# Macaron transformer on one core: exponential, scan and weight rests of the feed-forwards' routing rearranged

## Chip, cores and metric

One Trainium2 chip (trn2), one of its cores. The metric is device time in microseconds of one execution. Engines: TensorE (PE, its weight loads PEld), VectorE (DVE), ScalarE (ACT), GpSimd (POOL), SyncE (SP, which issues the DMAs here).

## What is computed

A tensor of 8 x 512 tokens with 128 channels passes six residual blocks: F0, A0, F0 (layer 0), F1, A1, F1 (layer 1). Each adds its result to x, the feed-forwards with a factor of 0.5. The change touches the four feed-forwards.

```python
# layer 0: gated, 8 experts and 2 shared, hidden 256, the best 2 of 8
shared = sum(_ffn(xf, sw1[i], sw2[i], sw3[i]) for i in range(2))
logits = xf @ router_w.T + expert_bias
rw, sel = jax.lax.top_k(logits, 2)
rw = jax.nn.softmax(rw, axis=-1)
combine = jnp.einsum('tk,tke->te', rw, one_hot(sel, 8))
out = shared + sum(combine[:, e] * _ffn(xf, w1[e], w2[e], w3[e]))   # silu(x w1) * (x w3) w2

# layer 1: relu squared, 8 experts, hidden 512, the best 2 of 8, with a capacity
oh_t = one_hot(top_idx, 8).transpose(1, 0, 2).reshape(2 * N, 8)      # N = 4096 tokens
pos = jnp.cumsum(oh_t, axis=0)
rank = jnp.sum((pos - 1) * oh, axis=-1)
valid = rank < 1280
out = sum over k of expert_out[top_idx[k]] * softmax(top_logits)[k] * valid[k]
```

## The kernel before

The program is a row of phases, P (loads, first norm), F0a, A0, F0b, F1a, A1, F1b; all engines but SyncE meet at a barrier between two phases (`barrier`, line 115), and each engine's instructions stand in an order written out by hand. Order between engines comes from semaphores alone. x lies in SBUF as `X` (32 tiles of 128 tokens) and transposed as `XT`.

`ffn_phase` (line 851) builds a feed-forward. It has a routing stage and then a loop over 8 chunks of 512 tokens.

Routing, on VectorE (`route_vector`, line 531): 32 tiles x 8 logits, 256 elements per partition, are handled at once. Two rounds (lines 539 to 551) find the largest and the second largest logit; the difference of the two maxima goes into `ex` (line 558); the one-hots are cast to bf16 (`oh_b`, line 560). `route_scalar` (line 602) takes the exponential on ScalarE; lines 563 to 567 make the two probabilities of it. In layer 1, TensorE counts with two matmuls (`route_tensor`) how many tokens of a tile went to each expert, and VectorE sums these counts with eight scans of 64 elements, one per expert (line 577), forms ranks and masks by the capacity (lines 580 to 589). Lines 594 to 598 weight, add the two choices and halve the sum, which gives `cw`. TensorE transposes `cw` (`turn_weights_tensor`, line 620), ScalarE copies it out (`keep_weights_scalar`, line 626; in layer 1 with a square root), and SyncE writes it to memory (line 520) and reads it back repeated over the partitions as `cwb`, half a chunk at a time (line 526). The routing's scratch lies in `cwb` itself in layer 1, and in `dn1` in layer 0.

Products are kept near fp32 precision by splitting each operand into a top part and a rest (three matmuls for each product): `XS` holds both parts of a chunk of XT, `dn_hi`/`dn_lo` those of the down weights, `up1_hi`/`up1_lo` those of layer 1's up weights, whose raw form is loaded by DMA at the phase's start into the buffer `h`. In the kernel before, ScalarE makes the top parts of the weights (lines 906 and 908) ahead of the exponential, and GpSimd makes both parts of the first XS (`split_gpsimd`, lines 230 and 232) and all rests of weights (lines 930 and 933).

The loop: TensorE runs three matmuls for an up-projection (lines 251 to 253; six in layer 0), and, `LAG` columns later, three for the down-projection (268 to 270), each waiting for its semaphore in order. In layer 0, ScalarE applies Silu (line 330), VectorE multiplies (408), GpSimd multiplies with `cwb` (477), ScalarE and VectorE split the result (322, 401). In layer 1, VectorE takes relu times `cwb` (line 445) and so needs `cwb` for its first column, ScalarE squares and copies (359, 364), VectorE subtracts (431), and GpSimd does both parts for every fourth column. GpSimd also splits the next chunk's XS. `norm_scalar` (lines 176, 177) copies a transposed chunk twice, into `xT_c` and into XT, and `norm_logits_tensor` (line 164) waits for both copies before its matmuls (line 168) read `xT_c`.

Of the kernel before, what the change touches and what calls it, by code (L numbers as in the profile page):

```python
# [34 lines left out]
def macaron(nc, x, alpha, w_qkv0, bias_rows0, wo0, wo0_t, wfc0, router0, expert_bias, up0, down0,  # L35
            w_qkv1, wo1, router1, up1, down1, out, stop_after=99):
    ctx = ExitStack()
    with ctx:
# [37 lines left out]
        dn_top, dn_split = sem("dn_top"), sem("dn_split")  # L76
        weights_out = sem("weights_out")
# [86 lines left out]
        def norm_logits_tensor(eng, s, i, lay, bank=7):  # L164
            eng.wait_ge(s["xt_copied"], 2 * i + 4)
            eng.wait_ge(s["lg_copied"], i + 1)
            for t in range(TPC):
                last = eng.matmul(ps[:, bank, t * E:(t + 1) * E], xT_c[:, t * P:(t + 1) * P], rw[lay][:, :],
                                  start=True, stop=True)
            last.then_inc(s["lg_done"], 1)  # L170
# [63 lines left out]
        def ffn_tensor(eng, s, lay, XS, hl, yT, w_hi, w_lo, dn_hi, dn_lo, nxt):  # L234
# [21 lines left out]
            def down(c, p, done, j):  # L256
                e, hb = divmod(j, HB)
                n = c * N + j
                if lay == 0:
                    eng.wait_ge(s["lo_done"], n + 1)  # L260
                elif on_pool(j):
                    eng.wait_ge(s["lo_pool"], c * pool_part(N) + pool_part(j + 1))
                else:
                    eng.wait_ge(s["lo_done"], c * own_part(N) + own_part(j + 1))
                if j == 0 and done == 2:
                    eng.wait_ge(s["x_added"], c - 1)
# [40 lines left out]
        def gated_scalar(eng, s, h, hl, yT, nxt):  # L307
# [4 lines left out]
            eng.preload_act_table(ACT.Silu)  # L312
# [150 lines left out]
        def gated_gpsimd(eng, s, XS, h, cwb, loads, nxt):  # L463
# [3 lines left out]
            def chunk(c, p, done):  # L467
                if done:
                    eng.wait_ge(s["up_done"], c * N)
# [15 lines left out]
        def squared_gpsimd(eng, s, XS, h, hl, nxt):  # L485
# [3 lines left out]
            def chunk(c, p, done):  # L489
                if done:  # L490
                    eng.wait_ge(s["up_done"], c * N)
# [39 lines left out]
        def route_vector(eng, buf, n, lay, m0):  # L531
            work, oh, oh_b, m, ex, pr, rank, tot, cum, incr = buf
# [5 lines left out]
            for k in range(2):  # L538
                eng.tensor_reduce(m[:, k, :], src[:, :, :], AX.X, ALU.max)
                eng.drain()  # L540

# [26 lines left out]
            eng.drain()  # L568
            if lay == 1:
# [17 lines left out]
                for k in range(2):  # L587

                    eng.scalar_tensor_tensor(out=oh[:, k].rearrange("p t e -> p (t e)"),
                                             in0=rank[:, k].rearrange("p t e -> p (t e)"), scalar=float(CAP),  # L590
                                             in1=oh[:, k].rearrange("p t e -> p (t e)"), op0=ALU.is_lt, op1=ALU.mult)
# [5 lines left out]
            eng.drain()  # L597
            eng.tensor_scalar(cw[:, :, :, :].rearrange("p c e t -> p c t e"),
                              work[:, 2].rearrange("p (c t) e -> p c t e", t=TPC), 0.5, None, ALU.mult)
            eng.drain().then_inc(step, 1)  # L600

        def route_scalar(eng, buf, n):
            ex = buf[4]
            eng.wait_ge(step, n + 2)
# [26 lines left out]
        def route_buffers(scratch, oh_b):  # L631
            taken = [0]

            def b(*shape):
# [5 lines left out]
                if len(shape) == 2:  # L640
# [3 lines left out]
                    b(E, 2, TILES), b(E, 2 * TILES), incr]  # L644
# [206 lines left out]
        def ffn_phase(name, lay, nxt):  # L851
# [9 lines left out]
            with ExitStack() as st:  # L861
# [17 lines left out]
                def body(block):  # L879
# [13 lines left out]
                    def _(eng):  # L893
# [4 lines left out]
                        eng.wait_ge(dn_split, number + 1)  # L898
                        ffn_tensor(eng, s, lay, XS, hl, yT, w_hi, w_lo, dn_hi, dn_lo, nxt)
# [18 lines left out]
                    def _(eng):  # L918
                        route_vector(eng, buf, n0, lay, m0)
# [28 lines left out]
        def attn0():  # L948
# [10 lines left out]
            with ExitStack() as st:  # L959
# [43 lines left out]
                def body(block):  # L1003
# [299 lines left out]
                    def _(eng):  # L1303
# [77 lines left out]
                        def chunk(c, p, done):  # L1381
                            first = done == 0
                            for n in range(UNITS):
# [43 lines left out]
                                if n == 5:  # L1427
                                    norm_logits_tensor(eng, s, c, nxt, SPARE)
# [18 lines left out]
                        for n in range(LAST):  # L1447
# [9 lines left out]
                            if n == 5:  # L1457
                                norm_logits_tensor(eng, s, B, nxt, SPARE)
# [7 lines left out]
                        norm_logits_tensor(eng, s, B + 1, nxt, SPARE)  # L1466
# [688 lines left out]
```

## Time and profile before

| | us |
|---|---|
| median of 3 runs | 3185.7 |
| lowest, highest | 3185.64, 3187.7 |
| profiled execution | 3189.26 |
| its span, first to last instruction | 3187.5 |

| engine | busy us | share of the span |
|---|---|---|
| PE | 2611.3 | 82% |
| PEld | 1734.8 | 54% |
| DVE | 2328.8 | 73% |
| ACT | 2261.4 | 71% |
| POOL | 1904.3 | 60% |

The page's shares are means over seven phases with different limits. What a routing stage costs has to be read from the stretch between a phase's barrier and its first up-projection, by engine. Times in a trace are from the span's start. In a row of the timeline, the brackets at its end tell how long the engine was idle before it and who released it.

### The profile page before, as it was taken

The page shows a single profiled execution, that of the slowest core. Times are in us where ns is not written, and L with a number is a line of the kernel's source. Part 1 is how long each engine was busy: PE and PEld are TensorE (multiplying, and loading weights), DVE is VectorE, ACT ScalarE, POOL GpSimd, SP SyncE. Part 2 cuts the span into 40 slices and gives each one's busy share as a digit, 9 for nine tenths or more (in the row PEclk, how much of TensorE's full clock was granted, in tenths as well). Part 3 has the DMA queues.
Part 4 walks back from the last instruction along what each step waited for, and adds up shares of the span by engine and source line. Part 5 has one row for each costly group of instructions (what it writes and reads, how often), then busy time and mean ns, then how long its engine had stood idle before and what let it go on. Part 6 is the DMA issues. An engine that isn't in the chain of part 4 may idle for free. (4 is left out here: it accounts for less than half of the span.)

```text
span 3187.5 us, 42265 instructions
## 1 busy us (share of the span) xinstructions
PE 2611.3 (82%) x12174; PEld 1734.8 (54%) x12208; DVE 2328.8 (73%) x4338; ACT 2261.4 (71%) x2559; POOL 1904.3 (60%) x1486
## 2 busy tenths in 40 slices
PE   4999958999789996799985778777787787469998
PEld 3877745555478774678872223232232232158887
DVE  5677746666466675898877687787787878378887
ACT  2555526777545554577764999999999999557776
POOL 2766667777456675444444666666766767344444
PEclk9999979999899998899996666676767666679999
DMA  3111100000011111111100000000000000111111
GB/s 114 54 40 53 39 1 1 2 1 1 1 55 54 53 39 66 55 54 40 45 21 1 0 0 1 1 1 1 1 1 1 1 1 1 53 51 44 53 39 53
DMA packets 13588, 86.72 MB, mean 27 GB/s; under 512 B 2176, under 2 KB 4224, under 8 KB 4224
## 3 DMA queue, kind: packets, MB, share of 16 engines
q1 hardware_dynamic: 13440, 84.96, 7.2%
q8 instruction: 67, 1.10, 0.1%
q14 instruction: 81, 0.66, 0.1%
HBM read 82.33 MB, written 2.62 MB: 27 GB/s over the span
## 5 line engine op out<-in xcount | busy, mean ns | idle before, releaser
L1743 POOL TENSOR_TENSOR A_Y<-A_Y,A_U 128x2048 f32<-128x2048 f32 x86 | 389.9, 4555 | 226.8 <-ACT A_U L1786 226.8
L1819 DVE TENSOR_SCALAR A_U<-ps 128x1024 f32<-128x1024 f32 x256 | 309.3, 1219 | 126.1 <-POOL A_Y L1743 62.4
L1825 DVE SCALAR_TENSOR_TENSOR A_U<-ps,A_U 128x1024 f32<-128x1024 f32 x256 | 311.4, 1216 | 58.2 <-PE ps L1955 58.2
L1955 PE MATMUL ps<-A_QT,A_KT 9*128 9x512 f32 x512 | 181.4, 705 | 195.8 <-DVE A_U L1825 163.3
L477 POOL TENSOR_TENSOR F0b_h<-F0b_h,dn 128x512 f32<-128x512 f32 x128 | 211.9, 1660 | 123.7 <-DVE F0b_h L408 123.5
L477 POOL TENSOR_TENSOR F0a_h<-F0a_h,dn 128x512 f32<-128x512 f32 x128 | 212.0, 1661 | 117.4 <-DVE F0a_h L408 117.2
L513 POOL TENSOR_TENSOR gated<-half_neg 128x1 f32<-128x1 f32 x179 | 37.7, 210 | 397.8 <-ACT F1a_h L359 178.3
L1743 POOL TENSOR_TENSOR dn<-dn,A_U 128x2048 f32<-128x2048 f32 x42 | 190.2, 4553 | 112.6 <-ACT A_U L1786 112.6
L1955 PEld LDWEIGHTS ps<-A_QT,A_KT 9*128 9x128 f32 x512 | 66.0, 254 | 335.5 <-DVE A_U L1825 238.4
L1265 DVE CUSTOM_DVE_ANT_0 ps<-ps,A_mask 128x256 f32<-128x256 f32 (+1 forms) x512 | 185.1, 423 | 84.4 <-PE ps L1335 78.8
L1786 ACT ACTIVATE A_U<-A_U 128x2048 f32<-128x2048 f32 (+1 forms) x96 | 236.5, 2464 | 0.0
L1927 PE MATMUL ps<-A_Y,A_VA 128*32 128x512 f32 x688 | 229.1, 800 | 5.8 <-DVE A_OT L1725 3.0
L445 DVE SCALAR_TENSOR_TENSOR F1b_h<-ps,F1b_cwb 128x512 f32<-128x512 f32 x256 | 176.1, 688 | 51.9 <-PE ps L253 34.4
L330 ACT ACTIVATE F0b_h<-ps 128x512 f32<-128x512 f32 x160 | 95.8, 599 | 161.7 <-PE ps L253 161.7
L359 ACT ACTIVATE F1a_h<-F1a_h 128x512 f32<-128x512 f32 x256 | 158.3, 625 | 71.9 <-DVE F1a_h L445 70.9
L1044 POOL TENSOR_SCALAR A_KZ<-A_KT,A_own 128x512 fp32r<-128x512 f32 x132 | 204.5, 1566 | 5.6 <-issue 5.6
L330 ACT ACTIVATE F0a_h<-ps 128x512 f32<-128x512 f32 x160 | 95.8, 599 | 155.4 <-PE ps L253 155.4
L359 ACT ACTIVATE F1b_h<-F1b_h 128x512 f32<-128x512 f32 x256 | 161.0, 629 | 61.6 <-DVE F1b_h L445 57.4
L1944 PE MATMUL ps<-A_QT,A_KT 28*128 28x512 f32 x512 | 167.5, 671 | 42.2 <-DVE A_U L1819 38.2
L1785 ACT ACTIVATE A_Y<-A_U 128x2048 f32<-128x2048 f32 (+1 forms) x64 | 159.4, 2490 | 51.6 <-DVE A_U L1825 51.4
L445 DVE SCALAR_TENSOR_TENSOR F1a_h<-ps,F1a_cwb 128x512 f32<-128x512 f32 x256 | 173.0, 684 | 24.9 <-PE ps L253 15.2
L408 DVE TENSOR_TENSOR F0b_h<-F0b_h,ps 128x512 f32<-128x512 f32 x160 | 109.9, 687 | 103.1 <-ACT F0b_h L330 102.5
(365 smaller groups left out, 8366.6 us busy)
## 6 DMA issues: line engine op xcount, KB each, us to landing
dn<-weight_rows SPq DMA_DIRECT2D x32, 1024.0 KB, 4.7
F1a_cwb<-weight_rows SPq DMA_DIRECT2D x16, 1024.0 KB, 4.7
F1b_cwb<-weight_rows SPq DMA_DIRECT2D x16, 1024.0 KB, 4.7
dn<-in_down SPq DMA_DIRECT2D x2, 2048.0 KB, 12.1
stage<-in_up SPq DMA_DIRECT2D x1, 2560.0 KB, 9.4
X<-in_x SPq DMA_DIRECT2D x1, 2048.0 KB, 8.4
F1a_h<-in_up SPq DMA_DIRECT2D x1, 2048.0 KB, 7.5
F1b_h<-in_up SPq DMA_DIRECT2D x1, 2048.0 KB, 7.7
```

Source lines behind the costliest of these rows:

```text
L330: eng.activation(h[:, j % ring, :], ps[:, (j * G) % 4, :], ACT.Silu).then_inc(s["pre_done"], 1)
L359: eng.activation(z, z, ACT.Square).then_inc(s["sq_done"], 1)
L445: eng.scalar_tensor_tensor(out=h[:, j % ring, :], in0=ps[:, j % 4, :], scalar=0.0, in1=cwb[:, j // HB, :], op0=ALU.max, op1=ALU.mult).then ...
L477: eng.tensor_tensor(z, z, cwb[:, r // HB, :], ALU.mult).then_inc(s["weighed"], 1)
L1044: last = eng.tensor_scalar(KZ[:, g % 2, j, :], KT[:, g, :].bitcast(F32), own[:, j:j + 1], None, ALU.mult)
L1265: last = eng.tensor_tensor_reduce(part, part, mask[:, w0:w1], -1.0, 3e38, ALU.add, ALU.min, QA[:, p, t, 4 * g + 2 * i + b, 3 * HD:3 * HD + ...
L1743: eng.tensor_tensor(flat(y_slot(m, h)), flat(y_slot(m, h)), flat(Um[:, h % UR]), ALU.add).then_inc(s["t_ready"], 1)
L1786: eng.activation(u, u, ACT.Sqrt).then_inc(s["s_ready"], 2 if joined else 1)
L1819: eng.tensor_scalar(u_step(n), d_pair(n), 0.0, None, ALU.max).then_inc(s["dp_vector"], 1)
L1825: eng.scalar_tensor_tensor(out=u, in0=g_pair(), scalar=CLAMP, in1=u, op0=ALU.min, op1=ALU.mult).then_inc(s["u_ready"], 1)
L1927: last = eng.matmul(ps[j:j + 32, OUT, :], VA[:, v0:v0 + 32], y_slot(m, h)[:, kt, :], start=(kt == 0), stop=(kt == TPC - 1))
L1955: last = eng.matmul(ps[:, 4 + b, :], KT[r:r + 9, pair, kt * P:(kt + 1) * P], QT[r:r + 9, pair, :], start=True, stop=True)
```

## The change

- `ex`, the difference of the maxima, is computed inside the second round, and its semaphore step comes there.
- ScalarE's order in a feed-forward becomes: table load for Exp, copy of the first chunk into XS, (layer 0: copy of dn_hi), exponential, table load (Sqrt or Silu), (layer 1: copies of up1_hi and dn_hi when their DMAs are in), copy of the turned weights.
- VectorE makes, after the whole routing, the rests of XS, of up1 (layer 1) and of the down weights; GpSimd makes none of them. GpSimd's first `split_gpsimd`, for the second chunk, waits for the first up-projection.
- The eight scans become one over 512 elements, whose multiplier is 0 at each expert's first element and 1 elsewhere (`restart`, set by GpSimd at the start of a layer 1 phase).
- Casts to `oh_b` are made in layer 1 alone. The weighting multiplies move ahead of the wait for TensorE's counts; the capacity mask is applied to their result. The halving moves into line 563, where it costs no instruction, and line 598 goes.
- TensorE waits for `dn_split` at its first down-projection instead of ahead of the loop.
- `norm_logits_tensor` waits for the first of the two copies only, in the feed-forwards.

```diff
-        def norm_logits_tensor(eng, s, i, lay, bank=7):
-            eng.wait_ge(s["xt_copied"], 2 * i + 4)
+        def norm_logits_tensor(eng, s, i, lay, bank=7, copies=1):
+            eng.wait_ge(s["xt_copied"], 2 * i + 2 + copies)
...
+                if j == 0 and done == 0:
+                    eng.wait_ge(dn_split, number + 1)
...
             def chunk(c, p, done):
-                if done:
-                    eng.wait_ge(s["up_done"], c * N)
+                eng.wait_ge(s["up_done"], c * N if done else 1)
                 split_gpsimd(eng, s, XS, (c + 1) % B, 1 - p)
...
+                if k == 1:
+                    eng.tensor_tensor(ex[:, 0, :], m[:, 1, :], m[:, 0, :], ALU.subtract).then_inc(step, 1)
...
-            eng.tensor_tensor(ex[:, 0, :], m[:, 1, :], m[:, 0, :], ALU.subtract).then_inc(step, 1)
-            for k in range(2):
-                eng.tensor_copy(oh_b[:, k].rearrange("p e t -> p t e"), oh[:, k])
+            if lay == 1:
+                for k in range(2):
+                    eng.tensor_copy(oh_b[:, k].rearrange("p e t -> p t e"), oh[:, k])
             eng.drain().then_inc(step, 1)
             eng.wait_ge(step, n + 3)
-            eng.tensor_scalar(ex[:, 2, :], ex[:, 1, :], 1.0, None, ALU.add)
+            eng.tensor_scalar(ex[:, 2, :], ex[:, 1, :], 1.0, 2.0, ALU.add, ALU.mult)
...
+            for k in range(2):
+                eng.tensor_tensor(work[:, k], oh[:, k], be(pr[:, k, :]), ALU.mult)
             if lay == 1:
                 eng.wait_ge(step, n + 4)
...
-                for e in range(E):
-                    eng.tensor_tensor_scan(cum[:, e, :], ones_f[:, 0:2 * TILES], tot[:, e].rearrange("p k t -> p (k t)"),
-                                           0.0, ALU.mult, ALU.add)
+                eng.wait_ge(restart_ready, n_restart)
+                eng.tensor_tensor_scan(cum[:, :, :].rearrange("p e n -> p (e n)"), restart[:, 0, :],
+                                       tot[:, :, :, :].rearrange("p e k t -> p (e k t)"), 0.0, ALU.mult, ALU.add)
...
-            for k in range(2):
-                eng.tensor_tensor(work[:, k], oh[:, k], be(pr[:, k, :]), ALU.mult)
             eng.drain()
-            eng.tensor_tensor(work[:, 2], work[:, 0], work[:, 1], ALU.add)
-            eng.drain()
-            eng.tensor_scalar(cw[:, :, :, :].rearrange("p c e t -> p c t e"),
-                              work[:, 2].rearrange("p (c t) e -> p c t e", t=TPC), 0.5, None, ALU.mult)
+            eng.tensor_tensor(cw[:, :, :, :].rearrange("p c e t -> p c t e"),
+                              work[:, 0].rearrange("p (c t) e -> p c t e", t=TPC),
+                              work[:, 1].rearrange("p (c t) e -> p c t e", t=TPC), ALU.add)
...
                     @block.scalar
                     def _(eng):
+                        eng.preload_act_table(ACT.Exp)
+                        eng.activation(XS[:, 0, 0, :], XT[:, 0:S], ACT.Copy).then_inc(xs_top, 1)
+                        if lay == 0:
+                            eng.activation(dn_hi[:, :, :, :], dn_raw[:, :, :, :], ACT.Copy).then_inc(dn_top, 1)
+                        route_scalar(eng, buf, n0)
                         if lay == 1:
+                            eng.preload_act_table(ACT.Sqrt)
                             eng.wait_ge(load["up1"], 16 * load_number)
                             eng.activation(w_top, w_raw, ACT.Copy).then_inc(up1_top, 1)
                             eng.wait_ge(load["dn1"], 16 * load_number)
-                        eng.activation(dn_hi[:, :, :, :], dn_raw[:, :, :, :], ACT.Copy).then_inc(dn_top, 1)
-                        route_scalar(eng, buf, n0)
+                            eng.activation(dn_hi[:, :, :, :], dn_raw[:, :, :, :], ACT.Copy).then_inc(dn_top, 1)
+                        else:
+                            eng.preload_act_table(ACT.Silu)
                         keep_weights_scalar(eng, cw_t, m0, lay)
...
                     @block.vector
                     def _(eng):
-                        route_vector(eng, buf, n0, lay, m0)
+                        route_vector(eng, buf, n0, lay, load_number)
+                        eng.wait_ge(xs_top, number + 1)
+                        eng.tensor_tensor(XS[:, 0, 1, :], XT[:, 0:S], XS[:, 0, 0, :].bitcast(F32),
+                                          ALU.subtract).then_inc(s["split_done"], 1)
+                        if lay == 1:
+                            eng.wait_ge(up1_top, load_number)
+                            eng.tensor_tensor(w_rest, w_raw, w_top.bitcast(F32), ALU.subtract).then_inc(up1_split, 1)
+                        eng.wait_ge(dn_top, number + 1)
+                        eng.tensor_tensor(dn_lo[:, :, :, :], dn_raw[:, :, :, :], dn_hi[:, :, :, :].bitcast(F32),
+                                          ALU.subtract).then_inc(dn_split, 1)
...
                     @block.gpsimd
                     def _(eng):
                         if lay == 1:
-                            eng.wait_ge(up1_top, load_number)
-                            eng.tensor_tensor(w_rest, w_raw, w_top.bitcast(F32), ALU.subtract).then_inc(up1_split, 1)
-                        split_gpsimd(eng, s, XS, 0, 0)
-                        eng.wait_ge(dn_top, number + 1)
-                        eng.tensor_tensor(dn_lo[:, :, :, :], dn_raw[:, :, :, :], dn_hi[:, :, :, :].bitcast(F32),
-                                          ALU.subtract).then_inc(dn_split, 1)
+                            flags = buf[9][:, 0, :]
+                            eng.memset(flags, 1.0)
+                            eng.drain()
+                            eng.memset(flags.rearrange("p (e n) -> p e n", e=E)[:, :, 0:1], 0.0)
+                            eng.drain().then_inc(restart_ready, 1)
```

## Rows read from the trace of the kernel before

**Rows 1.** Stages: stretch, us, busy us of PE, PEld, DVE, ACT, POOL, clock, DMA share, GB/s.
```profile
50.40:67.40 17.00, 0.00 (x0) 0.00 (x0) 14.84 (x22) 2.57 (x2) 9.52 (x5) 1.00 0.00 0
1251.80:1290.40 38.60, 0.63 (x1) 0.13 (x2) 25.68 (x36) 10.03 (x5) 21.22 (x6) 0.50 0.27 109
1640.00:2776.70 1136.70, 824.33 (x3217) 342.74 (x3215) 851.67 (x995) 1021.75 (x414) 721.88 (x441) 0.68 0.00 1
2776.70:2815.70 39.00, 0.63 (x1) 0.13 (x2) 26.97 (x37) 8.63 (x4) 21.22 (x6) 0.50 0.27 108
2824.40:3187.00 362.60, 352.92 (x1556) 291.21 (x1556) 307.98 (x456) 279.28 (x456) 167.99 (x206) 0.98 0.13 49
```

**Rows 2.** Timeline of DVE in F0a: start, us, engine, line, operation, idle before.
```profile
51.07 0.42 DVE L539 TENSOR_REDUCE dn<-logits 128x32 f32<-128x256 f32 x1 [0.63 <-PEq L651]
...
53.98 5.34 DVE L548 TENSOR_TENSOR dn<-dn 128x256 f32<-128x256 f32 x1
...
63.15 1.27 DVE L560 CAST F0a_r_ohb<-dn 128x256 bf16<-128x256 f32 x2
64.75 0.18 DVE L563 TENSOR_SCALAR dn<-dn 128x32 f32<-128x32 f32 x1 [0.32 <-ACT dn L605]
...
67.03 0.40 DVE L598 TENSOR_SCALAR cw<-dn 128x256 f32<-128x256 f32 x1
...
71.43 0.69 DVE L408 TENSOR_TENSOR F0a_h<-F0a_h,ps 128x512 f32<-128x512 f32 x1 [4.00 <-ACT F0a_h L330]
```

**Rows 3.** Timeline of POOL in F0a's routing.
```profile
53.47 5.57 POOL L933 TENSOR_TENSOR F0a_dn_lo<-dn,F0a_dn_hi 128x2560 fp32r<-128x2560 f32 x1 [0.34 <-ACT F0a_dn_hi L908]
```

**Rows 4.** Timeline of PE in F0a: its first up-projection matmul.
```profile
67.86 0.78 PE L251 MATMUL ps<-F0a_xs,up_lo 128*128 128x512 f32 x1
```

**Rows 5.** Timeline of DVE in F1a.
```profile
1252.42 0.42 DVE L539 TENSOR_REDUCE F1a_cwb<-logits 128x32 f32<-128x256 f32 x1 [0.65 <-PEq L651]
...
1257.41 0.42 DVE L548 TENSOR_TENSOR F1a_cwb<-F1a_cwb 128x256 f32<-128x256 f32 x1
...
1270.00 2.48 DVE L563 TENSOR_SCALAR F1a_cwb<-F1a_cwb 128x32 f32<-128x32 f32 x1 [10.71 <-ACT F1a_cwb L605]
...
1274.08 11.74 DVE L577 TENSOR_TENSOR_SCAN F1a_cwb<-ones_f,F1a_cwb 128x64 f32<-128x64 f32 x8
...
1298.27 1.89 DVE L445 SCALAR_TENSOR_TENSOR F1a_h<-ps,F1a_cwb 128x512 f32<-128x512 f32 x3 [7.88 <-DMA F1a_cwb<-weight_rows]
```

**Rows 6.** Timeline of ACT in F1a.
```profile
1264.81 3.62 ACT L908 ACTIVATE F1a_dn_hi<-dn 128x4096 fp32r<-128x4096 f32 x1 [1.27 <-DMA dn<-in_down]
1268.45 1.28 ACT L605 ACT_TABLE_LOAD   x1
1269.74 0.23 ACT L605 ACTIVATE F1a_cwb<-F1a_cwb 128x32 f32<-128x32 f32 x1
...
1291.19 0.38 ACT L626 ACTIVATE F1a_cw_t<-ps 128x256 f32<-128x256 f32 x1 [19.93 <-PE ps L620]
```

**Rows 7.** Line 577 in F1b: count, ns shortest/median/longest, first and last start.
```profile
L577 DVE TENSOR_TENSOR_SCAN F1b_cwb<-ones_f,F1b_cwb x8: 258/260/7952, 2800.4 to 2810.8; 128x64 f32<-128x64 f32 x8
```

**Rows 8.** Chain of waits through F1b's start: start, us, what.
```profile
2789.85 3.62 ACT F1b_dn_hi L908
...
2816.46 0.39 ACT F1b_cw_t L626
...
2824.39 0.70 DVE F1b_h L445
...
2831.06 0.43 PE ps L269
2831.48 0.23 PE ps L270
```

**Rows 9.** Timeline of DVE in P: the 5120-element subtraction.
```profile
44.61 5.49 DVE L841 TENSOR_TENSOR up_lo<-stage,up_hi 128x5120 fp32r<-128x5120 f32 x1 [1.35 <-ACT up_hi L809]
```

**Rows 10.** Timeline of PE at F0b's end: the last logits matmuls.
```profile
1249.67 1.87 PE L168 MATMUL ps<-rw,xT_c 128*128 128x8 f32 x8 [1.17 <-ACT XT L177]
```

More of the change, by code:

```diff
@@ L76, in macaron @@
         dn_top, dn_split = sem("dn_top"), sem("dn_split")
+        xs_top, restart_ready = sem("xs_top"), sem("restart_ready")
         weights_out = sem("weights_out")
@@ L232, in split_gpsimd, with ffn_tensor @@
             eng.tensor_tensor(lo, xt, hi.bitcast(F32), ALU.subtract).then_inc(s["split_done"], 1)
-        def ffn_tensor(eng, s, lay, XS, hl, yT, w_hi, w_lo, dn_hi, dn_lo, nxt):
+        def ffn_tensor(eng, s, lay, XS, hl, yT, w_hi, w_lo, dn_hi, dn_lo, nxt, number):
             U, HB, G = ffn_shape(lay)
@@ L311, in gated_scalar @@
                 norm_credits_scalar(eng, s)
-            eng.preload_act_table(ACT.Silu)
             def top(c, done, j):
@@ L489, in chunk @@
             def chunk(c, p, done):
-                if done:
-                    eng.wait_ge(s["up_done"], c * N)
+                eng.wait_ge(s["up_done"], c * N if done else 1)
                 split_gpsimd(eng, s, XS, (c + 1) % B, 1 - p)
@@ L528, in weights_sync, with route_vector @@
                         .then_inc(weights_in[half], 16)
-        def route_vector(eng, buf, n, lay, m0):
-            work, oh, oh_b, m, ex, pr, rank, tot, cum, incr = buf
+        def route_vector(eng, buf, n, lay, n_restart):
+            work, oh, oh_b, m, ex, pr, rank, tot, cum, restart = buf
             def be(a):
@@ L587, in route_vector @@
                 for k in range(2):
-                    eng.scalar_tensor_tensor(out=oh[:, k].rearrange("p t e -> p (t e)"),
+                    eng.scalar_tensor_tensor(out=work[:, k].rearrange("p t e -> p (t e)"),
                                              in0=rank[:, k].rearrange("p t e -> p (t e)"), scalar=float(CAP),
-                                             in1=oh[:, k].rearrange("p t e -> p (t e)"), op0=ALU.is_lt, op1=ALU.mult)
-                eng.drain()
-            for k in range(2):
-                eng.tensor_tensor(work[:, k], oh[:, k], be(pr[:, k, :]), ALU.mult)
+                                             in1=work[:, k].rearrange("p t e -> p (t e)"), op0=ALU.is_lt, op1=ALU.mult)
             eng.drain()
-            eng.tensor_tensor(work[:, 2], work[:, 0], work[:, 1], ALU.add)
-            eng.drain()
-            eng.tensor_scalar(cw[:, :, :, :].rearrange("p c e t -> p c t e"),
-                              work[:, 2].rearrange("p (c t) e -> p c t e", t=TPC), 0.5, None, ALU.mult)
+            eng.tensor_tensor(cw[:, :, :, :].rearrange("p c e t -> p c t e"),
+                              work[:, 0].rearrange("p (c t) e -> p c t e", t=TPC),
+                              work[:, 1].rearrange("p (c t) e -> p c t e", t=TPC), ALU.add)
             eng.drain().then_inc(step, 1)
@@ L603, in route_scalar @@
             ex = buf[4]
-            eng.wait_ge(step, n + 2)
+            eng.wait_ge(step, n + 1)
             eng.activation(ex[:, 1, :], ex[:, 0, :], ACT.Exp).then_inc(step, 1)
@@ L643, in route_buffers @@
             return [b(3, TILES, E), b(2, TILES, E), oh_b, b(3, TILES), b(3, TILES), b(2, TILES), b(2, TILES, E),
-                    b(E, 2, TILES), b(E, 2 * TILES), incr]
+                    b(E, 2, TILES), b(E, 2 * TILES), b(1, E * 2 * TILES)]
         out_w1 = sb("out_w1", [P, D])
@@ L897, in _ @@
                             eng.wait_ge(up1_split, load_number)
-                        eng.wait_ge(dn_split, number + 1)
-                        ffn_tensor(eng, s, lay, XS, hl, yT, w_hi, w_lo, dn_hi, dn_lo, nxt)
+                        ffn_tensor(eng, s, lay, XS, hl, yT, w_hi, w_lo, dn_hi, dn_lo, nxt, number)
                         barrier(eng, b0)
@@ L1427, in chunk @@
                                 if n == 5:
-                                    norm_logits_tensor(eng, s, c, nxt, SPARE)
+                                    norm_logits_tensor(eng, s, c, nxt, SPARE, 2)
                                 if n == 6:
@@ L1457, in _ @@
                             if n == 5:
-                                norm_logits_tensor(eng, s, B, nxt, SPARE)
+                                norm_logits_tensor(eng, s, B, nxt, SPARE, 2)
                         eng.wait_ge(s["lg_copied"], B + 2)
@@ L1465, in _ @@
                         norm_turn_tensor(eng, s, B + 1, SPARE)
-                        norm_logits_tensor(eng, s, B + 1, nxt, SPARE)
+                        norm_logits_tensor(eng, s, B + 1, nxt, SPARE, 2)
                         barrier(eng, b0)
```

## Prediction

> **What bounds the kernel now.** I read the stage table first, to see where TensorE stands still, then the timelines of those stages, then the chain of waits through one of them. The four feed-forward phases each open with a routing stage in which TensorE does nothing of weight: 17.0 us in F0a (F0b repeats it, instruction for instruction), 38.6 us in F1a, 39.0 us in F1b [rows 1]. Behind it the loops over the chunks are TensorE's: 352.92 of 362.60 us busy in F1b [rows 1], with back-to-back matmuls of 0.23 us at full clock [rows 8]. So whatever the prologue is shortened by, TensorE's first up-projection starts earlier and the phase ends earlier by the same amount; nothing in the loop can take it back, since the loop's own pace is unchanged.
>
> In the prologue the reader should see two kinds of lost time. First, lock-like stalls on VectorE. In F0a line 548 takes 5.34 us, from 53.98 to 59.32 [rows 2], and its twin in F1a takes 0.42 us [rows 5]; GpSimd's subtraction for dn_lo runs from 53.47 to 59.04 [rows 3], and the stalled instruction ends 0.28 us after it. In F1 the same happens to line 563 (2.48 us for 32 elements) and to the first of the eight scans (11.74 us for the group in F1a [rows 5]; in F1b one scan is 7952 ns where the shortest is 258 ns [rows 7]). Second, the exponential: in the F1 phases it stands on ScalarE's queue behind two copies of 3.62 us that wait for the weights' DMAs, the second of which ends at 1268.43 in F1a [rows 6] and 2793.47 in F1b [rows 8]; VectorE idles 10.71 us for it in F1a [rows 5].
>
> The Trainium skill, SBUF — State Buffer, section "Who interferes with whom", says that a VectorE instruction with two SBUF inputs and a GpSimd instruction that reads SBUF exclude each other for a whole instruction, and that the one issued first wins. By that rule the 5.34 us are 0.42 of work and the rest waiting; the rows agree to 0.28 us.
>
> **The change, part by part.**
>
> *GpSimd leaves the routing (all phases).* Its two weight subtractions and the first chunk's split go to VectorE and ScalarE, and its first split now waits for the first up-projection. So both rounds of the arg-max run as they do in F1a, where GpSimd was idle: line 539 starts at 1252.42, line 548 of round two ends at 1257.83, 5.41 us [rows 5]. The difference `ex` (32 elements, about 0.26 us with its gap, an estimate between line 563's 0.18 [rows 2] and a 256-element 0.42) now stands inside it: 5.7 us.
>
> *F0a.* Before: 51.07 to the end of line 598 at 67.43, 16.4 us [rows 2]. After: 5.7, no casts of oh_b (line 560, 1.27 us, on the path as TensorE doesn't use them here), no wait for the exponential (see below), then lines 563 to 596, which are 64.75 to 67.03 less a gap, 2.3 us [rows 2]; line 598 (0.40 and its gap) is folded into the addition. That is 8.0 us, so cw stands at 59.1 instead of 67.43: 8.35 us earlier. TensorE then waits for VectorE's new XS subtraction, 512 elements: by line 841, 5.49 us for 5120 elements [rows 9], 1.07 ns per element, so 0.55 and an overhead: 0.7 us where the old start came 0.34 us behind the transposes' start and needed nothing. Cost 0.45. The dn_lo subtraction (2560 elements, 2.75 us by the same rate) runs from 59.9 to 62.7; TensorE only asks for it at the first down-projection, and VectorE's own next work, line 408, came 3.57 us behind TensorE's first matmul (67.86 [rows 4] to 71.43 [rows 2]), so 60.0 plus 3.57, 63.5: covered by 0.8 us. Were the cover gone it would cost at most 2.75. Gain of F0a: 7.9 us. Bounds 6.5 to 8.4.
>
> ScalarE's new order in F0a is table load, XS copy, dn_hi copy, exponential. Two of its durations stand in the stage row (2.57 us for the dn_hi copy and the exponential [rows 1]); with a 512-wide copy of about 0.6 (an estimate from 3.62 us for 4096 elements and an overhead) and a table load of 1.28 [rows 6] it is done some 4.5 us in, at 55.5, while VectorE asks for it at 56.8. In hand: 1.3 us. The Trainium skill, ScalarE: Activation LUTs, "What ACT_TABLE_LOAD costs", gives 1283 ns for the load and another 1380 ns of drain; by it the exponential would come at 56.9, and the sum would be 0.1 us worse per F0 phase. Against it stands that the load in F1a began 0.02 us behind a copy and ended where the exponential began, at 1269.74 [rows 6].
>
> *F0b.* Same instructions, same stalls, 7.9 us. Further, the last logits matmul waits for one copy instead of two: it stood at 1249.67 behind line 177's copy [rows 10], and now starts one overlapped copy, 0.5 us, earlier. In the loop this wait is hidden behind TensorE's queue. 8.4 us.
>
> *F1a.* Two rounds 5.7 from 1252.42, casts 1.27 (they feed TensorE's two ranking matmuls here): 1259.4. The exponential now needs only the copy of XS ahead of it and is done about 1256.5; no wait. The tail before, from line 563's end at 1272.48 to the stage's end at 1290.4 [rows 1], was 17.9 us, of which 11.74 are scans [rows 5]: 6.2 left, less 0.5 for line 598, plus 0.2 for an unstalled line 563, is 5.9. The one scan over 512 elements: no row shows one. A 512-wide plain pass at 1.07 ns is 0.7; eight times the shortest scan is 8 x 0.258 [rows 7] = 2.1. I take 1.2, as the shortest scan stands above a plain instruction of its size and eight fixed costs become one. Routing ends at 1259.4 + 5.9 + 1.2 = 1266.6 instead of 1290.4. TensorE's ranking matmuls run beside the weighting multiplies, which are moved in front of the wait for just that.
>
> Now what is next late. (a) ScalarE: its copy of dn_hi holds it until 1268.43 [rows 6], so the weights leave then and not at 1267.3; from line 626's start to line 445's start were 7.08 us (1291.19 [rows 6] to 1298.27 [rows 5]), two DMAs through memory: weights there at 1275.5. (b) VectorE: after 1266.6 come 0.7 for XS, 4.4 for up1's rests and 4.4 for dn_lo (4096 elements each at 1.07 ns): free at 1276.2. Both subtractions lie beside the weights' travel, as (a) and (b) tie within 1 us. (c) TensorE starts its ups once up1's rests are there, at 1271.7, and has the first four banks full 12 x 0.43 us later [rows 8], at 1276.9, while line 445 needs them one by one; not late. Line 445 starts at 1276.3 against 1298.27: 22.0 us. The restart flags are two GpSimd memsets at the stage's start, 10 us ahead of the scan; they cost nothing unless they hold up VectorE's first instructions, at most 1 us.
>
> *F1b.* Same routing, 14.2 us, from 2777.3 (its stage begins at 2776.7 [rows 1]): cw at 2791.5. ScalarE is free only at 2793.47 [rows 8], and from line 626 to line 445 were 7.93 us (2816.46 to 2824.39 [rows 8]): weights at 2801.4; VectorE free at 2801.1. Gain 2824.39 - 2801.4 = 23.0 us.
>
> *TensorE's clock.* Before, TensorE filled its banks, stalled for the weights, and then ran 0.43 us per matmul (1.2 GHz) until 2831.3, when it rose to 0.23 us (2.4 GHz) [rows 8]. Now the filling ends just as line 445 begins, so the clock should be up by then. From 2825.1 to 2831.3 are 14 matmuls, 3.3 us at full clock: 2.8 us to be had at most, none at least. The ramp of the first columns through ScalarE and VectorE takes part of it back; I take 1.0 in each F1 phase.
>
> **Sum.** 7.9 + 8.4 + 23.0 + 24.0 = 63.3 us. The profiled execution was 3189.3 us (span 3187.5) and would be 3126.0; the median of the runs shown is 3.6 us lower, so 3185.7 - 63.3 = 3122.4 us.
>
> **Rivals.**
> *1. The weights' travel becomes the bound and is longer than before.* The row loads now follow the 2 MB loads by 4 to 10 us instead of 25. Line 626 to 445 took 7.08 and 7.93 us; two to four us more in each F1 phase gives 3126 to 3131. For: only the travel is now behind ScalarE's last copy in F1b. Against: the weights' loads have landed by then (2789.85 [rows 8]). Chance 0.12.
> *2. GpSimd's postponed split collides with VectorE.* By the rule cited above the two block one another, and GpSimd's pair of instructions is 1.98 us (9.52 less 5.57, for two pairs [rows 1, 3]). It becomes ready one up-projection into dn_lo's subtraction, is held until that ends, and then may hold VectorE's first hl rest: up to 1.3 us in each F1 phase, 3125. Without the rule nothing. Chance 0.10.
> *3. The stalls are not GpSimd's.* Then lines 548 and 577 keep their long instructions: F0 gains 2 us each, F1 some 12 each, total 28, 3158 us. Against it the matched ends (0.28 us). Chance 0.03.
> *4. Slower: the clock is granted less in F1b.* F1b follows A1, in which the granted clock was 0.68 over 1136.7 us; F1b had 0.98 [rows 1]. The changed F1b begins its TensorE work 19 us sooner behind A1 and without the pause. If it were held at 0.68, its 362.6 us would be 362.6 x 0.98/0.68 = 522, plus 160, net 3282. It decides once the loop's mean falls below 0.98 x 362.6/(362.6+63) = 0.83. Against: in F1b the clock rose 15.6 us after the routing stage's end (2815.7 [rows 1] to 2831.3 [rows 8]), stall included. Chance 0.02.
> *5. The exponential or the flags hold the routing after all* (ScalarE's table loads, late flags): 1 us in each phase, 3126. Chance 0.05.
> *6. More than summed*: the whole clock term and a shorter travel, 67 to 70 us, 3116 to 3119. Chance 0.10.
>
> **How the numbers follow.** Forecast, 3119 to 3126: 0.58. Rivals 1, 2, 5 and 6 lie between 3116 and 3131, together 0.37; 3 and 4 lie far away. The bounds of the terms add up to some 55 to 69 us. The range takes them in with a little: 3114 to 3133. What a measurement can tell from no change is 0.2%, 6.4 us, a tenth of the gain; only rival 4 crosses it: faster 0.97, same 0.01, slower 0.02.
>
> **What would show it.** In the changed profile: no VectorE instruction of the routing over 1 us but the scan and the casts; line 548's twin 0.42 in F0a; the exponential ended before VectorE reaches its wait; TensorE's first up-projection 8 us earlier relative to the stage's start in F0, and the first use of the weights 22 to 23 us earlier in F1, with about 0.2 us between VectorE's last subtraction and it. Wrong would be: a VectorE wait of several us for the weights' DMA behind the subtractions (rival 1), rests of hl over 1 us at the loop's start (2), 0.43 us matmuls far into a loop (4).

## The result

The changed kernel takes 3134.5 us (median of 4 runs, 3131.6 to 3135.5) against 3186.1 us before (median of 4): a ratio of 0.9835, 95% interval 0.9822 to 0.9848, or 51.7 us less. The forecast was 3122.4 us, 63.3 us less. Its profiled execution took 3135.5 us (before 3189.3), span 3133.8. One execution of one kernel below (b_vector_rests) took 4715.4 us in a slower state and enters no comparison.

What was forecast for the routing stages came to within half a microsecond. The stage table of the changed kernel, columns as in [rows 1]:

```profile
50.40:59.20 8.80, 0.03 (x1) 0.03 (x1) 6.85 (x18) 5.54 (x5) 0.00 (x0) 1.00 0.00 0
1235.90:1250.80 14.90, 1.07 (x3) 0.17 (x3) 12.59 (x30) 8.56 (x6) 0.64 (x2) 0.50 0.70 282
2747.80:2763.10 15.30, 1.08 (x3) 0.18 (x3) 12.61 (x30) 9.10 (x6) 0.64 (x2) 0.50 0.68 275
```

From the barrier to the finished `cw`, 17.0, 38.6 and 39.0 us [rows 1] have become 8.8, 14.9 and 15.3 us, and GpSimd is idle in them but for the flags (0.64 us in each layer 1 stage). VectorE in F0a and in F1a (timeline: start, us, engine, line, operation, idle before), answering [rows 2] and [rows 5]:

```profile
56.10 0.42 DVE L550 TENSOR_TENSOR dn<-dn 128x256 f32<-128x256 f32 x1
...
63.54 0.69 DVE L410 TENSOR_TENSOR F0a_h<-F0a_h,ps 128x512 f32<-128x512 f32 x1 [0.91 <-ACT F0a_h L332]
...
1236.57 0.42 DVE L539 TENSOR_REDUCE F1a_cwb<-logits 128x32 f32<-128x256 f32 x1 [0.65 <-PEq L651]
...
1246.00 1.22 DVE L581 TENSOR_TENSOR_SCAN F1a_cwb<-F1a_cwb 128x512 f32<-128x512 f32 x1
...
1250.05 0.62 DVE L597 TENSOR_TENSOR cw<-F1a_cwb 128x256 f32<-128x256 f32 x1
1250.79 0.69 DVE L927 TENSOR_TENSOR F1a_xs<-XT,F1a_xs 128x512 fp32r<-128x512 f32 x1
1251.40 4.42 DVE L931 TENSOR_TENSOR up_lo<-F1a_h,up_hi 128x4096 fp32r<-128x4096 f32 x1
1255.74 4.42 DVE L933 TENSOR_TENSOR F1a_dn_lo<-dn,F1a_dn_hi 128x4096 fp32r<-128x4096 f32 x1
1260.07 1.88 DVE L447 SCALAR_TENSOR_TENSOR F1a_h<-ps,F1a_cwb 128x512 f32<-128x512 f32 x3
```

No routing instruction is held (line 550 is 0.42 us where its twin took 5.34), and the first use of the weights comes 1260.07 - 1236.57 = 23.5 us behind the routing's first instruction, where it was 45.85 us [rows 5]. VectorE comes to it with no idle time: its own rests were the last, the weights were there.

The missing time is in F1a. From VectorE's first routing instruction of one feed-forward to that of the next (and to the span's end), in us:

| kernel | F0a and A0 | F0b | F1a and A1 | F1b |
|---|---|---|---|---|
| before | 816.6 | 384.8 | 1524.9 | 410.2 |
| changed | 808.5 | 377.1 | 1511.9 | 385.3 |
| gained | 8.1 | 7.7 | 13.0 | 24.9 |
| forecast | 7.9 | 8.4 | 23.0 | 24.0 |

F1a's prologue gained 22.35 us (45.85 less 23.5), and its first addition to x came 22.5 us earlier. The two phases together gained 13.0, so 9.5 us were given back behind it: 8.3 in F1a's loop, as follows, and 1.2 behind F1a's last addition (1115.5 us up to F1b's routing, before 1114.3), nearly all of it A1. The starts of VectorE's addition to x (line 380, after it 382) stand 45.5 us apart all through F1a's loop before, and 45.5, 45.6, **49.6**, 45.5, **49.8**, 45.5 us in the changed kernel. VectorE and TensorE in the first long one:

```profile
1439.17 0.69 DVE L447 SCALAR_TENSOR_TENSOR F1a_h<-ps,F1a_cwb 128x512 f32<-128x512 f32 x1 [1.81 <-PE ps L254]
1442.63 0.69 DVE L433 TENSOR_TENSOR F1a_hl<-F1a_h,F1a_hl 128x512 fp32r<-128x512 f32 x1 [2.77 <-issue]
...
1443.38 0.50 PE L271 MATMUL ps<-F1a_hl,F1a_dn_lo 128*128 128x512 f32 x1 [2.14 <-DVE F1a_hl L433]
```

```profile
1437.75:1441.00 3.25, 3.25 (x16) 2.55 (x14) 0.69 (x1) 1.01 (x2) 2.87 (x4) 1.00 0.88 323
1441.00:1443.40 2.40, 0.26 (x3) 0.02 (x1) 0.77 (x2) 0.25 (x1) 0.87 (x1) 1.00 0.01 3
1443.40:1447.40 4.00, 4.00 (x11) 3.15 (x12) 4.00 (x7) 3.26 (x6) 0.25 (x1) 0.57 0.00 0
```

"<-issue" is the row to see: VectorE stands 2.77 us and waits for nothing that the profile shows. TensorE runs out of work for 2.14 us, and its granted clock then is 0.57 over 4 us (mostly 1.2 GHz) where it was 1.00. The period is 4.1 us longer in all; how much of that is the clock is shown by b_pad117 below. It happens at each of the two jumps back of VectorE's chunk loop, which holds 300 instructions of the program.

### The profile page after: what moved, and what is told of

Same layout as the page of the kernel before. It is cut to its first block and busy times, and to the rows that moved or that the text cites. A ratio compares the mean times of both kernels' runs of the same rounds, so it can differ in the third digit from the quotient of the medians.

```text
span 3133.8 us, 42282 instructions
## 1 busy us (share of the span) xinstructions
PE 2620.4 (84%) x12208; PEld 1739.4 (56%) x12208; DVE 2308.5 (74%) x4326; ACT 2266.4 (72%) x2566; POOL 1857.2 (59%) x1476
```

## Experiments

### Is it the place of the code?

The change leaves VectorE with 11 instructions fewer ahead of F1a's loop. Five kernels shift VectorE's code and nothing else, by semaphore increments at its head in phase P (the number stands in the name); a sixth writes its loops out.

```diff
                 @block.vector
                 def _(eng):
+                    for _i in range(16):
+                        eng.sem_inc(spare, 1)
                     eng.wait_ge(load["x"], 16)
```

> The changed kernel with 16 semaphore increments put at the head of VectorE's queue in phase P, where it idles 9.16 us for x. They do no work and only shift all later VectorE code by 16 instructions. Theory A (code position): in the changed kernel VectorE stands still for 2.8 us with nothing to wait for at each of the two jumps back in F1a's chunk loop, and instruction packets of 8192 bytes are loaded there; the shorter code ahead of the loop (11 instructions) has moved the loop across one more block boundary. 16 more put it back: the two stalls go, all chunk periods of F1a are 45.5 us, F1a with A1 is 8 us shorter, and the kernel takes some 3126 us. Theory B (the stalls come from the new order of work itself, say from cwb's loads or GpSimd's postponed split): nothing changes, 3134 us.

Measured: 3123.1 us, ratio 0.9802 (0.9786 to 0.9818). Every period of F1a's loop is 45.5 or 45.6 us, and no wait for "issue" is left there. F0a starts where it did (50.98 us, 51.01 without the increments), so the increments themselves cost nothing. The theory of the code's position holds, the new order of the work isn't the cause.

> The same with 100 increments. Two versions of theory A differ here. A1, blocks of 128 instructions (8192 bytes, the size of the instruction packets on the queue that serves VectorE; 64 bytes each) of which a loop can use three: the loop's start falls at 89 to 99 in a block of 128, 300 instructions then touch four blocks, the stalls stay: 3134 us. A2, the page Runtime: NRT and Kernel Launch of the Trainium skill, section Instruction fetch mechanics, which has blocks of 256 instructions and two of them at hand: 300 instructions from 89 to 99 touch two blocks, no stall: 3126 us. Theory B: 3134 us, and then a_pad16 also.

Measured: 3125.0 us, 0.9806 (0.9790 to 0.9823), periods 45.9 us at the jumps. As a time that looks like the expectation's version A2 (blocks of 256), but the DMA view says otherwise. Two queues carry instructions: q8 has 67 packets in every kernel here, and q14 has 81 before and 91 in the changed kernel and changes with VectorE's code. Instruction packets on q14, over the last three chunk periods of F1a's loop (columns: packets, MB, share of the DMA engines), in the changed kernel, in a_pad100, in a_pad118 and in a_pad128, the same line in each:

```profile
q14 instruction: 6, 0.05, 0.1%
```

For the same stretch of a_pad16 and of the kernel before, the view has no instruction packet at all. So with 100, blocks of the loop are loaded anew in each turn too, and only the price is lower: 0.4 us for each jump. (F0a starts 1.1 us later here, for the increments.)

> The kernel before with 117 increments at the same place, which put F1a's VectorE loop at the same place in a block of 128 as the changed kernel has it (11 short of before's), and far from a boundary of 256. A1: the kernel before gets the same two stalls, F1a's periods become 45.5 and twice 49.7 us, 3186 + 8 = 3194 us. A2 and B: 3186 us. The increments themselves are hidden behind the 9.16 us wait.

Measured: 3196.0 us, 1.0028 (1.0018 to 1.0037), periods 49.6 and 48.3 us at the jumps, six instruction packets. The kernel before can be given the changed kernel's loss. 2.8 of the 9.3 us are the increments (117 take longer than the idle time for x, 9.2 us; F0a starts at 53.9 instead of 51.1), which the expectation had as hidden.

The second of its jumps tells what the clock cost. VectorE and TensorE there, and the four us behind it (columns as in [rows 1]):

```profile
1576.83 0.69 DVE L432 TENSOR_TENSOR F1a_hl<-F1a_h,F1a_hl 128x512 fp32r<-128x512 f32 x1 [2.83 <-issue]
...
1577.58 0.50 PE L269 MATMUL ps<-F1a_hl,F1a_dn_lo 128*128 128x512 f32 x1 [2.17 <-DVE F1a_hl L432]
```

```profile
1577.50:1581.50 4.00, 3.92 (x17) 3.28 (x18) 4.00 (x8) 3.16 (x6) 0.14 (x1) 1.00 0.00 0
```

Both engines stand as long as in the changed kernel, but the granted clock stays at 1.00, and the period is 2.8 us longer and not 4.1. So the stop itself costs 2.8 us and the fallen clock some 1.3 more. It fell behind the other five such stops (the changed kernel's, a_pad128's and b_pad117's first: 0.57 to 0.67 over 4 us); why not behind this one stays open.

> The changed kernel with 128 increments at VectorE's head. If the period of the block is 128 instructions (8192 bytes), F1a's loop stands as in the changed kernel itself and its two long periods (49.6 and 49.8 us) come back: 3134 us and at most 1 to 3 us more for the increments. If the period is 256, or the position doesn't matter, periods of 45.5 us and 3124 us.

Measured: 3138.6 us, 0.9845 (0.9828 to 0.9861), periods 49.9 and 49.4 us. F0a starts 3.9 us later for the increments; without them it is the changed kernel's time. The stalls come back after 128 instructions. By the times alone a divisor of 128 would do as well; the packets of 8192 bytes speak for 128.

> The changed kernel with 118 increments: F1a's loop starts 10 instructions earlier in its block than in the changed kernel, so 11 to 21 ahead of the next block boundary, where the changed kernel stands 1 to 11 ahead of it (4.1 us for each jump back) and a_pad100 29 to 39 ahead (0.4 us, though the blocks are loaded again there too). Theory A1, refined: the loop touches four blocks in all three, and what is lost depends on how soon behind the jump's target the next block, which isn't there either, is needed. So the two long periods lie between 45.9 and 49.8 us, by the distance nearer the long end: 48 to 49 us, 3131 us. If the cost is one of yes or no by the number of blocks, 49.7 or 45.5 us.

Measured: 3127.9 us, 0.9812 (0.9796 to 0.9828), of which 3.0 us are the increments (F0a starts at 54.05), periods 45.9 and 46.3 us, though the blocks are loaded again. The expected 48 to 49 us was wrong: 10 instructions from the place where a jump costs 4.1 us, nearly all of the price is gone. VectorE at the same jump in a_pad118:

```profile
1440.56 0.69 DVE L448 SCALAR_TENSOR_TENSOR F1a_h<-ps,F1a_cwb 128x512 f32<-128x512 f32 x1 [1.85 <-PE ps L255]
1441.17 0.68 DVE L434 TENSOR_TENSOR F1a_hl<-F1a_h,F1a_hl 128x512 fp32r<-128x512 f32 x1
```

Both kernels idle some 1.8 us at the jump. The row names TensorE, but in a_pad16, which loads nothing, the longest wait around there is 0.49 us, so this is most likely the load of the target's block; TensorE's lead covers it. Only the changed kernel has a second stop at this jump, 2.77 us, one instruction later (a_pad118 has one of 0.59 us at its other jump). That a second block is missing there fits the packets; why 10 instructions more between target and block boundary hide nearly all of it was not measured.

One rival can be set aside from the traces. SyncE's row loads for `cwb` fill the DMA engines just as the blocks are fetched (share 0.88 from 1437.75 to 1441.00 above), so the stop might be a queue behind them. But VectorE also stands 2.38 us at A0's jump, where the share is 0.02:

```profile
636.44 0.36 DVE L1279 CUSTOM_DVE_ANT_0 ps<-ps,A_mask 128x192 f32<-128x192 f32 x1 [2.38 <-issue]
```

```profile
634.00:637.00 3.00, 2.69 (x19) 1.50 (x19) 0.62 (x4) 1.53 (x4) 0.00 (x0) 1.00 0.02 5
```

The row loads can be at the root of a few tenths of the 2.77 us, not of the stop.

The Trainium skill, Runtime: NRT & Kernel Launch, "Instruction fetch mechanics", has this mechanism: sequential prefetch, and a taken jump whose target isn't at hand stalls for a DMA. It gives blocks of 16 KiB or 256 instructions, two at hand. For VectorE the runs differ: packets of 8192 bytes (0.05 MB for six) and a period of 128. A count of the instructions gives the loop's start in its block up to a constant, and 11 values of that constant make all runs fit one rule: where the loop touches three blocks of 128 nothing is loaded again, where it touches four it is. A0's loop has 481 instructions on VectorE and so always touches four or more, which fits its stops in both kernels. A1's loop has 673 and yet shows no wait for "issue" over 0.3 us in the changed kernel; why was not followed up.

The loops written out on VectorE (A0, F1a, F1b):

```diff
-        def all_chunks(eng, chunk):
+        def all_chunks(eng, chunk, flat=False):
             chunk(0, 0, 0)
             chunk(1, 1, 1)
+            if flat:
+                for c in range(2, B):
+                    chunk(c, c % 2, 2)
+                return
...
-            all_chunks(eng, chunk)
+            all_chunks(eng, chunk, True)
...
-                        all_chunks(eng, chunk)
+                        all_chunks(eng, chunk, True)
```

> The changed kernel with VectorE's chunk loops of A0, F1a and F1b written out (no jump back on VectorE; the other engines keep theirs). Theory A: no jump, no stall. F1a's two go (8.2 us), and the two of 2.35 us in A0, which both kernels have, go too, worth up to 4.7 us: 3121 to 3126 us. Theory B: 3134 us.

Measured: 3120.3 us, 0.9792 (0.9775 to 0.9808), the fastest here, 66 us under the kernel before. F0a and A0 take 803.9 us where the changed kernel took 808.5; 4.0 of the 4.6 us lie behind F0a's last addition to x, so that is what A0's two stops, which both kernels have, were worth.

### The parts of the change

> The kernel before with one part of the change: ex inside the second round and the exponential ahead of ScalarE's weight copies. GpSimd keeps the rests, the eight scans stay. Theory L (VectorE and GpSimd exclude each other): VectorE no longer idles 10.71 and 9.39 us for the exponential in F1, but reaches GpSimd's two long subtractions earlier and is held by them instead: its two-input instructions behind the scans meet line 930 (8.8 us), which starts at the same time as before, and then line 933 (8.8 us). cw comes only some 3 to 5 us earlier in each F1 phase, F0 is unchanged: 3186 - 8 = 3178 us. Rival (the stalls aren't GpSimd's, rival 3 of the prediction): the whole idle time is gained, 10.7 + 9.4 us: 3166 us.

Its core, on the kernel before (`ex` is also computed inside the second round, as in the changed kernel):

```diff
+                        eng.preload_act_table(ACT.Exp)
+                        if lay == 0:
+                            eng.activation(dn_hi[:, :, :, :], dn_raw[:, :, :, :], ACT.Copy).then_inc(dn_top, 1)
+                        route_scalar(eng, buf, n0)
                         if lay == 1:
                             eng.wait_ge(load["up1"], 16 * load_number)
...
-                        route_scalar(eng, buf, n0)
```

Measured: 3179.9 us against 3188.0, 0.9973 (0.9962 to 0.9983). VectorE and GpSimd in F1a:

```profile
1260.20 1.57 DVE L578 TENSOR_TENSOR_SCAN F1a_cwb<-ones_f,F1a_cwb 128x64 f32<-128x64 f32 x8
...
1263.78 8.66 DVE L590 SCALAR_TENSOR_TENSOR F1a_cwb<-F1a_cwb 128x256 f32<-128x256 f32 x2
1272.51 10.28 DVE L595 TENSOR_TENSOR F1a_cwb<-F1a_cwb 128x256 f32<-128x256 f32 x2
```

```profile
1262.58 8.82 POOL L934 TENSOR_TENSOR up_lo<-F1a_h,up_hi 128x4096 fp32r<-128x4096 f32 x1 [17.48 <-ACT up_hi L911]
...
1273.52 8.98 POOL L937 TENSOR_TENSOR F1a_dn_lo<-dn,F1a_dn_hi 128x4096 fp32r<-128x4096 f32 x1
```

The wait for the exponential is gone and the two engines' mutual exclusion has taken its place: two pairs of 256-element instructions take 8.66 and 10.28 us, and GpSimd's instructions end at 1271.40 and 1282.50, each just ahead of its pair. The eight scans, met by nothing now, take 1.57 us where they took 11.74 [rows 5].

> The kernel before with the other part: XS top on ScalarE, all rests on VectorE behind the routing, GpSimd idle in the routing, dn_split asked for at the first down-projection. The exponential stays behind ScalarE's weight copies, the eight scans and the casts stay. Theory L: F0 loses its 6.5 us of stalls for 0.45 us of XS, 6 us each. In F1 the exponential still ends at 17.3 us into the stage (F1a), the tail behind it is 17.9 - 9.6 = 8.3 us without stalls, then 9.5 us of rests, so the first use of the weights comes some 35 us into the stage where it was 45.9: 11 us in F1a, 13 in F1b. Sum 36: 3150 us. Rival: no stall goes, the rests come on top: slower than before, 3186 + 15 us.

```diff
 # VectorE, behind route_vector
+                        eng.tensor_tensor(XS[:, 0, 1, :], XT[:, 0:S], XS[:, 0, 0, :].bitcast(F32),
+                                          ALU.subtract).then_inc(s["split_done"], 1)
+                        if lay == 1:
+                            eng.tensor_tensor(w_rest, w_raw, w_top.bitcast(F32), ALU.subtract).then_inc(up1_split, 1)
+                        eng.tensor_tensor(dn_lo[:, :, :, :], dn_raw[:, :, :, :], dn_hi[:, :, :, :].bitcast(F32),
+                                          ALU.subtract).then_inc(dn_split, 1)
 # and the same lines away from GpSimd
```

Measured: 3151.4 us against 3188.0, 0.9882 (0.9862 to 0.9902). First addition to x, from the routing's start: 6.0 and 6.6 us earlier in F0a and F0b, 10.9 in F1a, 14.7 in F1b. This is the larger part, and the eight scans take 0.27 us each in it. The two alone give 8.1 and 36.6 us, 44.7 together. The whole gives 51.7, and 63.6 us in a_pad16, where, as in both of these, no block of F1a's loop is loaded again. So what is left of the change is worth 27.0 us behind this part, against the exponential's 8.1 alone: it pays in full only once GpSimd is out of VectorE's way. The 27.0 also hold the one scan, layer 0's casts, the halving and the wait for one copy; of these only the scan was tried by itself.

> The changed kernel with dn_lo given back to GpSimd (at once when dn_hi is there), and 19 increments ahead, which keep F1a's loop where a_pad16 has it (3123 us). Theory L: in F0 GpSimd starts at about 4.1 us into VectorE's routing and holds a two-input instruction of it for 5 us: 5 us later in F0a and F0b. In F1 dn_hi is ready while VectorE subtracts up1's rests; GpSimd waits for that to end, then takes 8.8 us where VectorE took 4.4; VectorE's first use of the weights (one input in PSUM) isn't held, but its first rest of hl is, some 2.5 us. Sum 10 + 5: 3138 us. Rival: no exclusion; VectorE is freed of 2.75 and 4.4 us of work and the time is at or under 3123 us.

```diff
 # GpSimd, ahead of its loop
+                        eng.wait_ge(dn_top, number + 1)
+                        eng.tensor_tensor(dn_lo[:, :, :, :], dn_raw[:, :, :, :], dn_hi[:, :, :, :].bitcast(F32),
+                                          ALU.subtract).then_inc(dn_split, 1)
 # and the same lines away from VectorE
```

Measured: 3139.9 us, 0.9847 (0.9831 to 0.9864), 16.8 us over a_pad16. In F0a:

```profile
54.86 5.77 POOL L950 TENSOR_TENSOR F0a_dn_lo<-dn,F0a_dn_hi 128x2560 fp32r<-128x2560 f32 x1 [32.57 <-ACT F0a_dn_hi L909]
...
55.27 0.42 DVE L549 TENSOR_REDUCE dn<-dn 128x32 f32<-128x256 f32 x1
55.76 5.15 DVE L551 TENSOR_TENSOR dn<-dn 128x256 f32<-128x256 f32 x1
```

The reduction, with one input, passes beside GpSimd's instruction in 0.42 us; the next one, with two, waits for its end (60.63) and takes 5.15. One input is no safe sign, though: line 563 in F1a before, a TENSOR_SCALAR with one, took 2.48 us [rows 5] and ended at 1272.48, with the subtraction that GpSimd held there:

```profile
1263.62 8.82 POOL L930 TENSOR_TENSOR up_lo<-F1a_h,up_hi 128x4096 fp32r<-128x4096 f32 x1 [17.45 <-ACT up_hi L906]
```

F0a's and F0b's first additions come 5.1 and 5.3 us later, F1's 3.4 us (2.5 were expected), all against a_pad16.

> The changed kernel with eight scans of 64 elements again instead of one of 512, and 9 increments ahead, which put F1a's loop where a_pad16 has it (3123 us). GpSimd is idle then, so the eight take 8 x 0.26 less overlaps, some 1.9 us, against 1.22 of the one: routing 0.7 us later in each F1 phase. In F1a ScalarE's copy of dn_hi hides part of that for the weights, but VectorE's rests follow directly: 0.7 us each, 3124.5 us, to be seen in the stages and hardly in the time.

Measured: 3125.5 us, 0.9799 (0.9783 to 0.9816). The first additions to x come 0.3 to 0.4 us later in F1, not 0.7: the eight take about 1.6 us undisturbed, the one 1.22. The one scan as such is worth under 1 us of the 51.7; what cost 10 us in F1a's old scans was GpSimd. Most of the rest of the 2.4 us over a_pad16 lies in A1, on which more below.

## Why the prediction was right, and where it failed

The number was wrong, by 12.1 us, and 1.5 us outside its range (3114 to 3133); most of the mechanism was right. Point by point:

- **GpSimd holds VectorE in the routing**: right. The 5.34 us went to 0.42, a_gpsimd_dnlo brought them back, a_eight_scans and b_vector_rests showed the scans innocent. Rival 3 is out.
- **F0a**: cw was forecast for 59.1, its instruction ended at 59.08; TensorE's first up-projection for 60.0, at 59.95; line 408 for 63.5, at 63.54. The exponential ended at 55.24, forecast 55.5. Gain 8.1 us with A0, forecast 7.9. The 56.9 that the Trainium skill, ScalarE: Activation LUTs, "What ACT_TABLE_LOAD costs", would have given, with a drain behind the table load, was not seen: the load ended at 52.25 and the copy of XS began at 52.27.
- **F0b**: 7.7 us where 8.4 were forecast; 8.6 in a_pad16.
- **F1a, F1b prologues**: routing 14.1 us in F1a and 14.5 in F1b (forecast 14.2), the scan 1.22 (1.2; the forecast called it a choice between 0.7 and 2.1, so the closeness is partly luck), the first use of the weights 23.5 and 23.9 us behind the routing's start (23.9 and 24.0). "(a) and (b) tie" was right as far as shown: VectorE's rests ended last.
- **The clock term**: 1.0 taken for each F1 phase. F1b's first addition to x came 24.8 us earlier relative to its stage, the first use of the weights 23.1: 1.7 us. In F1a 22.5 against 22.35: 0.2. The clock was up when the weights were first used, as forecast (1.00 from 1260.0 and from 2772.0 on); before, F1b ran its first 7 us behind them at 0.54, F1a its first 4 at 0.60. The sum of the two was right, the even split wasn't.
- **"Nothing in the loop can take it back, since the loop's own pace is unchanged"**: this is the step that failed. The loop's instructions were the same, their place in memory wasn't. It cost 8.3 us by the periods (4.1 and 4.2), and a_pad16, with the same work in the same order, took 3123.1 us, 0.7 from the forecast. The rest of the difference, 3.0 us, lies behind F1a's last addition, nearly all in A1: the F1a and A1 segment is 11.3 us shorter in a_pad16, of which the periods explain 8.2. That stretch takes 1112.5 to 1115.5 us in the twelve traces. Its cause stays open: a_eight_scans, whose VectorE code in A1 stands, by the count, where a_pad16's does, takes 1115.0 there and a_pad16 1112.5, so the place of VectorE's code isn't enough to explain it.
- **From the profiled execution to the median**: the forecast took 3.6 us off, as before; the changed kernel's two lie 1.0 us apart. Between profiled executions the miss is 9.5 us (3135.5 against 3126.0), and the other 2.6 of the 12.1 come from this step. By the same measure a_pad16's profiled 3123.2 is 2.8 us under the forecast's 3126.0, so its median's agreement to 0.7 us is in part luck.
- **Rival 1** (weights' travel): no; VectorE never waited for them. **Rival 2** (GpSimd's postponed split): the exclusion is there, but it fell on GpSimd, whose 0.61 us cast took 2.83:

```profile
1257.80 2.83 POOL L231 CAST F1a_xs<-XT 128x512 fp32r<-128x512 f32 x1 [20.52 <-PE ps L254]
1260.77 1.29 POOL L233 TENSOR_TENSOR F1a_xs<-XT,F1a_xs 128x512 fp32r<-128x512 f32 x1
```

  It ended at 1262.06, and VectorE's first rest of hl began at 1262.12, held 0.17 us by ScalarE and not by GpSimd. **Rival 4** (clock): the clock fell, but for some 4 us behind each stall in F1a, not in F1b. **Rival 5**: no.

The trace of before had what was needed to ask the question: a loop of 300 instructions that a jump repeats, and waits for "issue" of 2.5 and 2.4 us at A0's two jumps. The prediction read neither, and its range held no term for it.

## What to carry to other kernels

Two engines that exclude each other turn a saved wait into another one: take the off-path engine's long instructions out of the way first, then shorten the chain. In a kernel with run-time loops, a change ahead of a loop also moves the loop: count the instructions of each engine's loop, look for "<-issue" rows and instruction packets at the jumps in both profiles, and try the change with a few idle instructions ahead before judging it. Writing out the loops of an engine whose loop doesn't fit was the fastest form here; A1's loop (673 instructions on VectorE) stayed a loop and was not tried.

## What the runs showed of the hardware

- VectorE's code comes in packets of 8192 bytes, and the effect of its place has a period of 128 instructions (a_pad128). A 300-instruction loop that by the count touches four such blocks has blocks loaded again in every turn; how it lies decides between 0.4 us (a_pad100) and some 4 us (changed kernel) for each jump back.
- The first stop at such a jump is booked in the profile as a wait for TensorE (1.81 us); only comparison with a_pad16 (0.49 us at most) shows that it is something else, most likely the first load.
- A stop of 2.8 us on VectorE cost 4.1 where TensorE's 2.1 us of idle time was followed by a lower granted clock (0.57 over the next 4 us), and 2.8 where it stayed at 1.00 (b_pad117's second jump, 2.17 us idle).
- A semaphore increment on VectorE took 0.09 us: its first other instruction began at 10.56 us behind 100 of them and at 13.15 behind 128.
- GpSimd's two-input subtraction held VectorE's two-input instructions (5.15 to 5.34 us for 0.42) and a one-input TENSOR_SCALAR (2.48 for 0.18), and let a one-input reduction pass (0.42).
